# Attention kernel, transformer layer: when the probability-times-value matmuls are taken from their queue, every two key tiles with an early release at the end of a pair, or at every key tile with one fixed depth

## The reference

```python
def layer(x, Wqkv, bqkv, Wproj, bproj, W, b, V_r, C):     # x: (8, 2048, 1024) f32
    q, k, v = split(layernorm(x) @ Wqkv + bqkv)            # 16 heads of 64
    s = where(causal, q @ k.T * 64**-0.5, -inf)
    x = x + (softmax(s) @ v) @ Wproj + bproj
    h = layernorm(x)
    return x + h @ W.T + b + (h @ V_r) @ C.T
```

## Time and profile before

| | us |
|---|---|
| median of 2 runs | 859.95 (859.42 to 860.49) |
| the profiled execution, as timed | 861.58 |
| its span, slowest core (core 0) | 860.0 |
| spans of the 8 cores | 843.5 to 860.0 |
| TensorE busy, core 0 | 662.5 |
| ScalarE busy | 334.5 |
| VectorE busy | 288.8 |
| GpSimd busy | 186.6 |

### The profile page before, as it was taken

The page is one execution under the profiler, slowest core; times in us unless marked ns, Lnnn a source line. Parts: engine busy times, 40 slices in busy tenths (PEclk is TensorE's granted clock), DMA queues, the critical chain, the costliest instruction groups (busy, mean ns, idle before and its releaser), DMA issues.

```text
span 860.0 us, 10453 instructions; the slowest of 8 cores (843.5 to 860.0 us)
## 1 busy us (share of the span) xinstructions
PE 662.5 (77%) x3389; PEld 279.7 (33%) x3433; DVE 288.8 (34%) x717; ACT 334.5 (39%) x449; POOL 186.6 (22%) x304
## 2 busy tenths in 40 slices
PE   0399999999047778778787978878889897965566
PEld 0144444444032223333232323323333333332222
DVE  2543435302023433334324333232323323244442
ACT  0131413231004355545455554647575757500000
POOL 2000000000105424425233222222222223123212
PEclk9999999999555568888979979698989899968898
DMA  8990200000861000000101000010101010101001
GB/s 160 215 220 28 74 26 25 0 1 1 136 111 48 0 1 1 26 24 26 49 1 50 25 25 29 22 50 1 50 1 50 1 49 2 50 25 61 37 25 50
DMA packets 15125, 38.13 MB, mean 44 GB/s; under 512 B 3401, under 2 KB 3425, under 8 KB 15073
## 3 DMA queue, kind: packets, MB, share of 16 engines
q0 software_dynamic: 7616, 11.67, 8.8%
q1 hardware_dynamic: 7457, 25.79, 8.5%
HBM read 39.68 MB, written 8.39 MB: 56 GB/s over the span
## 4 chain that ended last, share of the span: by engine, by line
PE 63%; DVE 14%; issue 7%; ACT 6%; POOL 5%; DMA 4%; DVEq 1%; SPq 0%; ACTq 0%; POOLq 0%
PE ps_pv L403 14%; PE ps_sc L251 12%; PE ps_sc L420 8%; PE ps_pv L276 6%; PE ps_w L551 4%; PE ps_w L628 4%; PE ps_bf L235 4%; DVE wq_a L490 3%; PE ps_pv L628 3%; DMA xf_a<-wffn 3%; POOL xf_a L440 3%; ACT xf_a L429 2%; ACT xnt_a L429 2%; PE ps_sc L551 2%; POOL xnt_a L440 2%
## 5 line engine op out<-in xcount | busy, mean ns | idle before, releaser
L429 ACT ACTIVATE xf_a<-ps_sc 128x1024 bf16<-128x1024 f32 (+1 forms) x192 | 167.7, 893 | 131.6 <-PE ps_sc L420 130.2
L420 PE MATMUL ps_sc<-q_fm,k_fm 64*128 64x512 bf16 (+3 forms) x640 | 125.9, 408 | 47.7 <-ACT xf_a L429 25.7
L429 ACT ACTIVATE xnt_a<-ps_sc 128x1024 bf16<-128x1024 f32 (+3 forms) x128 | 112.6, 897 | 128.2 <-PE ps_sc L420 128.0
L403 PE MATMUL ps_pv<-xf_a,v_on 128*66 128x512 bf16 (+3 forms) x384 | 118.3, 398 | 14.0 <-POOL xf_a L440 9.3
L251 PE MATMUL ps_sc<-xnt_a,wq_a 128*128 128x512 bf16 x499 | 114.7, 386 | 1.6 <-DVE xnt_a L317 0.9
L440 POOL TENSOR_TENSOR xf_a<-xf_a,tri_sb 128x128 bf16<-128x128 bf16 x152 | 61.0, 428 | 202.0 <-ACT xf_a L429 201.5
L403 PE MATMUL ps_pv<-xnt_a,v_on 128*66 128x512 bf16 (+3 forms) x256 | 81.4, 405 | 7.4 <-POOL xnt_a L440 4.9
L440 POOL TENSOR_TENSOR xnt_a<-xnt_a,tri_sb 128x128 bf16<-128x128 bf16 x104 | 42.5, 432 | 179.5 <-ACT xnt_a L429 178.8
L420 PEld LDWEIGHTS ps_sc<-q_fm,k_fm 64*128 64x128 bf16 x640 | 30.8, 96 | 152.1 <-issue 148.9
L251 PEld LDWEIGHTS ps_sc<-xnt_a,wq_a 128*128 128x128 bf16 x512 | 50.1, 99 | 60.7 <-issue 4.8
L210 ACT ACTIVATE ln_t<-mv,eps_t 128x1 f32<-128x1 f32 x32 | 9.3, 290 | 143.3 <-DVE mv L205 143.1
(11 more groups left out here) (65 smaller groups left out, 590.0 us busy)
## 6 DMA issues: line engine op xcount, KB each, us to landing
xf_a<-x SPq DMA_DIRECT2D x32, 512.0 KB, 3.4
y<-xf_a SPq DMA_DIRECT2D x16, 512.0 KB, 2.7
wq_a<-wqkv POOLq DMA_DIRECT2D x3, 2048.0 KB, 39.7
wq_a<-wproj POOLq DMA_DIRECT2D x1, 2048.0 KB, 19.5
xf_a<-wffn POOLq DMA_DIRECT2D x4, 512.0 KB, 25.8
bias_a<-bqkv POOLq DMA_DIRECT2D x1, 512.0 KB, 56.6
bias_a<-bffn POOLq DMA_DIRECT2D x1, 512.0 KB, 58.7
bias_a<-bproj SPq DMA_DIRECT2D x1, 512.0 KB, 6.3
```

The lines of the kernel that those rows point to most:

```text
L403: e.matmul(ps_pv[hd][0:66, off * 128:512], v_on[:, ki2, 66 * hh:66 * hh + 66], chunkpair(cp)[:, hd * 512:hd * 512 + ncol], start=st, stop=sp),
L420: e.matmul(ps_sc[:, pp * 1024 + hd * 512 + off * 128: pp * 1024 + hd * 512 + 512], k_fm[hp:hp + 64, hc, ki * 128:(ki + 1) * 128], q_fm[hp: ...
L429: e.activation(chunkpair(cp).rearrange("p (a n) -> p a n", a=2) [:, :, 0:ncol], ps_sc[:, pp * 1024:(pp + 1) * 1024] .rearrange("p (a n) -> ...
```

## The change

`pop_pv` loses its argument and always pops down to 6 entries, and it is called in every step. So from step 3 on every step issues two of the matmuls of line 403, those of three steps before. The early releases at steps K-2 and K-1 are gone; the drain after the last `pump()` has six entries in place of two. In group 0 (K = 4), the entries of step 0 are popped after the scores of step 3, before after those of step 2.

```diff
-            def pop_pv(drain=False, cap=6):
+            def pop_pv(drain=False):
                 nonlocal m_pv_last
-                while len(pend) > cap or (drain and pend):
+                while len(pend) > 6 or (drain and pend):
...
                 gki += 1
-                if ki % 2 == 1:
-                    pop_pv(cap=2 if ki == K - 1 else 6)
-                elif ki == K - 2:
-                    pop_pv(cap=4)
+                pop_pv()
                 pump()
             pop_pv(drain=True)
```

## The result

The changed kernel takes 849.73 us (median of 9 runs) against 859.58 us before (8 runs). The ratio is 0.9877, 95% interval 0.986 to 0.9894: 10.6 us less, between 9.1 and 12.0. The forecast was 5 us less, 855.0; the time lies inside the outer range of 845 to 865 and just outside the prediction's own of 850 to 860, and the gain is twice what was forecast.

A forecast was written before the change was run, and what follows sets the result against it. No engine bounds the attention stage everywhere; the bound changes inside a pair between TensorE, ScalarE, GpSimd and VectorE. Terms of -4.1-0.7-0.6+0.4 = -5.0 us against the 859.95 us median gave 855.0, range 850 to 860, outer range 845 to 865.

The forecast's parts named there:

- Group 0: Third to eighth pair: scores of step 3 move into an idle wait, 0.68 us less each, 4.1 us in all.
- Groups 1 and 2: Pairs other than group 1's two without filler: no gain, since filler or contiguous GpSimd masks cover; 0.2 us either way each.
- rival C: Granted TensorE clock turns out better, shorter group 0 pairs shifting what follows: 847 to 838.5 us; chance 0.12.
- Full pairs: Group 3: late scores of step 13 delay the masks, 0.1 us longer in each of four pairs, 0.4 us in all.
- The small terms: Group 1's two pairs without filler gain 0.35 us each (0.7); group 3's four light pairs 0.15 each (0.6).
- rival A: Switches to the scores are paid at 28 split places, 0.26 us each, 7.3 us in all: 862 us; chance 0.15.
- Rival B: Late odd scores starve the masks in all 24 pairs of groups 1 to 3, 0.43 us each: 865 us; chance 0.08.

The follow-up runs named there:

- e1: The new pop_pv calls in group 0 alone, the old ones in groups 1 to 3, on the kernel before: 854.3 us, ratio 0.9931.
- e2: The new pop_pv calls in groups 1 to 3 alone, the old ones in group 0, on the kernel before: 856.0 us, ratio 0.996.
- e3: The kernel before with the new calls in group 0 and the even pairs of groups 1 to 3, old calls in odd pairs: 847.8 us, ratio 0.9867.
- e6: The kernel before with VectorE's two reads of ps_w cut to 64 of 512 columns, the rest not computed: 847.6 us, one run.
- e7: The changed kernel with VectorE's two reads of ps_w cut to 64 of 512 columns, the rest not computed: 835.6 us, one run.
- e9: The changed kernel with the early release at the last step alone (down to 2 at K-1): 851.5 us, ratio 0.9918.
- e10: The changed kernel with the early release at step K-2 alone (down to 4): 857.9 us, ratio 0.9987.
- e5: The kernel before with a pop in every step, both early releases kept (4 at K-2, 2 at K-1): 864.6 us, ratio 1.006.
- e11: The changed kernel with 8 entries kept in place of 6, in every step: 847.1 us, ratio 0.9857.
- e4: The kernel before with pops at odd steps only, always down to 6 entries, no early releases: 848.4 us, ratio 0.9862.
- e12: The kernel before with pops every step in even pairs (8 entries), at odd steps in odd pairs (6), no early releases: 836.3 us, ratio 0.9735.

## Why the prediction was half right

**Group 0: right.** Forecast 4.1 us, measured 5.1, and e1 alone gives the same 5.1 on its slowest core. Six pairs of core 0 lost 0.65 to 1.0 us each, and the first and second 0.2 or less. The cover, the contiguous masks and TensorE as the next bound came out as worked out; the clock of some of these pairs was a little better (0.57 of full in place of 0.53).

**Groups 1 and 2: the step that failed.** "In the other pairs of groups 1 and 2 filler lies beside these waits, or GpSimd is contiguous: nothing, with 0.2 us either way in a pair." For 14 pairs the sum put this term at nothing. With the 0.7 us for the two pairs of group 1, groups 1 and 2 were to gain 0.7 us and gained 9.6 on the slowest core, 5.2 on the mean over the cores. (The bounds, 0 to -7.3 and +1.7, also left out the 0.2 us a pair, up to 2.8 us.) The step asked only which wait ends last in a pair and took the clock in it as given. What the runs showed in its place is the clock: from PEclk, the slowest core's time at 1.2 GHz in these groups fell from 78 to 47 us. At the 0.3 to 0.4 us that each us at the low clock costs in pairs of one order (the light ones of group 3 below give the lower figure), that is 9 to 12 us; at equal clock the pairs together got no shorter. e2 shows that the order inside groups 1 to 3 does it, and e1 that the shorter group 0 does not. Over the cores' means the three groups have 79 us at the low clock with the new order, 94 with the early releases put back, 97 before.

One wait behind it was there to be read, in rows of a kind of pair that the prediction hadn't opened: the idle TensorE at an even step of a light pair of group 2, with no matmul to issue. With two matmuls in that wait the pair's PEclk went from 0.82 to 0.90 on all cores. It isn't the whole of it: e3 has the same order in this pair, and there its clock differs from core to core. The clock was on the list as rival C, at 0.12, with half of its way at 847 us; the time came out near that. But its reason, "for it: shorter pairs in group 0 shift everything behind them", is not what happened, as e1 shows. So C named the right term for a wrong reason.

**Full pairs: the right place, the wrong wait.** Forecast 0.1 us longer each from the masks; measured 1.2 to 1.8 on the mean, of which 1.1 to 1.2 at equal clock, and the rest is more time at 1.2 GHz. The masks' part was sound: from the scores of step 12 to the end of a full pair it takes 5.94 us before (25.33-19.39) and 6.01 now (26.44-20.43). But the prediction asked for each edit what hides it, and not what the four matmuls of line 403 had themselves been hiding: VectorE's read of `ps_w` between two fillers. e6 and e7 show it by taking the read away. The odd pairs of group 2 lose by the same order, 19.8 us where the clock is full, before 18.95; that it is the same wait there is likely and wasn't separated.

**The small terms.** The two pairs of group 1 without filler gained 1.1 us on core 0 and 0.4 on the mean (forecast 0.7). The third, fifth and seventh pair of group 3 are 0 to 0.3 us shorter at equal clock (the fifth 18.84, then 18.57), where 0.15 was forecast.

**Luck in the total.** That the time lies between 845 and 865 us says little for the sum. On the slowest core it missed 9 us of gain in groups 1 and 2 and 5.6 us of loss in group 3 (5.4 longer, where 0.2 less was forecast), and the two errors partly cancel.

**Switches between scores and the rest (rival A): not paid.** The 28 split places are there: on core 1, TensorE goes to the scores 241 times in groups 1 to 3 and not 213, four times more in each light pair of group 3. At 0.26 us each such a pair would be 1.0 us longer; at equal clock none is longer, and on the mean the second to fourth took 18.6, 18.5 and 18.9 us, before 18.8, 19.2 and 18.9. The thin cover held. The Trainium skill's rule on the drain at a change of tiling mode ("TensorEngine Tiling (Array Packing)", section "Tiling Modes") describes a cost that is there in the rows, 0.12 to 0.14 us an edge, but hidden.

**Rival B** asked for the 0.43 us of the late odd scores to come through in every pair of groups 1 to 3. In the full pairs 0.07 us of it did (the 6.01 against 5.94), and the light pairs got no longer.

**What stays open.** Why the order changes where TensorE falls to 1.2 GHz isn't settled. Over all executions and cores the whole kernel spends 187 us at the low clock (2x(1-clock) of the span); with the release at the last step (e9) it is 198, with the one before it (e10) 202 and with both (e5) 220, of which group 0's old order is 11 to 12 in the last two. So one by one they cost 11 and 4 us of it, and together 21. Neither the number of matmuls behind the last scores (e11) nor the place of the groups in time (e1) explains it. Nor does the time at the low clock alone rank the versions: e4, e11 and e12 have more of it than the changed kernel and are as fast or faster. The lengths of a group come in a few values that return on several cores (group 2 before: 160.3, 163.8 and 166.0), so it seems to be a pattern that locks in over several pairs; that is an argument, and no run tests it.

## What to carry to other kernels

Before work is moved in an engine's order, write down what it stands between: a stretch that looks like load may be the cover of another engine's read, as four matmuls were for `ps_w` here. Fill the steps that wait with the work that doesn't, and batch where the queue is already full: the best version does both, by the kind of pair. And where cores with the same program differ by 2% with their clock, take that difference as a term that the order can move. Look at all cores, not only the slowest: comparing the same pair on cores where it had the same clock tells what the order does by itself.

## What the runs showed of the hardware that had not been expected

A wait of TensorE that ends with VectorE's read showed as "issue" of the weight load (0.52 us at 685.16) and not under VectorE's name. The starts of the instructions show it. And the clock fell to 1.2 GHz in the first steps of the pairs of group 3 (all but its first pair, on core 0) though TensorE stood still for no longer than 1.05 us at a time there, before and after the change. The Trainium skill, page "TensorE: Matmul & The Clock Gate", section "A second HAM failure mode: psum-queue depth-cycling", describes a clock that goes back and forth when TensorE idles briefly and often between groups of matmuls; the traces here agree that it falls beside such waits. They also show that it need not. The third pair of group 3 in the changed kernel, on core 0 and on core 1:

```profile
603.99:623.37 19.38, 16.94 (x84) 5.51 (x82) 4.64 (x15) 14.45 (x18) 5.48 (x10) 0.82 0.00 0
606.55:623.72 17.17, 14.55 (x83) 5.04 (x80) 4.63 (x15) 14.18 (x18) 5.48 (x10) 1.00 0.00 0
```

The waits at its start are alike, 1.05 and 0.78 us on core 0 and 1.05 and 0.99 on core 1, and yet one falls and the other never leaves 2.4 GHz; that is 2.2 us in one pair, 0.3 us for each us at the low clock.
